# Cross attentions: maximum, subtraction, exponential and copy of turned weights on two PSUM banks at a time in place of one

## The reference

```python
scores = jnp.einsum('bhqd,bhkd->bhqk', qh, kh) / jnp.sqrt(jnp.float32(d_k))
attn = jax.nn.softmax(scores, axis=-1)
out = jnp.einsum('bhqk,bhkd->bhqd', attn, vh)
```

## Time and profile before

| | before |
|---|---|
| median of 3 runs | 1664.79 us (1664.47 to 1664.91) |
| profiled execution, its own time | 1663.43 us |
| its span | 1661.6 us |
| PE busy | 1302.8 us (78%) |
| DVE busy | 940.4 us (57%) |
| ACT busy | 737.3 us (44%) |
| POOL busy | 416.1 us (25%) |
| granted clock of PE, mean | 0.854 of full speed |

### The profile page before, as it was taken

One profiled execution on the slowest core, in us unless ns is written; L12 is line 12 of the kernel. 1 busy time (PEld: TensorE's weight loads), 2 busy tenths in 40 slices (PEclk: granted clock), 3 DMA queues, 4 the chain that ended last, 5 costly groups with the idle time before them and its releaser, 6 DMA issues. The chain is left out here.

```text
span 1661.6 us, 26970 instructions
## 1 busy us (share of the span) xinstructions
PE 1302.8 (78%) x9634; PEld 905.2 (54%) x9635; DVE 940.4 (57%) x2049; ACT 737.3 (44%) x1366; POOL 416.1 (25%) x435
## 2 busy tenths in 40 slices
PE   6997894468797975778778738693999768697998
PEld 3786463247464651346446527462677646365676
DVE  3687464767575456876775783485233367555111
ACT  2343552341462234675585534472455434163432
POOL 0222100013200015463463501300444335410000
PEclk9899797567797986879979967796999879798999
DMA  6000000200000000000000000510000000000000
GB/s 248 1 0 0 1 2 1 78 1 0 1 2 1 1 1 0 0 2 1 1 1 1 1 1 2 234 50 1 1 0 0 1 1 1 1 2 1 1 1 14
DMA packets 6340, 27.28 MB, mean 16 GB/s; under 512 B 1329, under 2 KB 4433, under 8 KB 5585
## 3 DMA queue, kind: packets, MB, share of 16 engines
q1 hardware_dynamic: 6224, 25.76, 3.9%
HBM read 25.23 MB, written 0.52 MB: 16 GB/s over the span
## 5 line engine op out<-in xcount | busy, mean ns | idle before, releaser
L745 DVE TENSOR_REDUCE L_xattn_top<-banks 128x4 f32<-128x512 f32 x128 | 80.7, 672 | 52.9 <-PE banks L603 52.9
L1188 DVE SCALAR_TENSOR_TENSOR L_ffn_a<-banks,L_ffn_act_out 128x512 f32<-128x512 f32 (+1 forms) x72 | 47.7, 662 | 103.5 <-POOL L_ffn_act_out L1118 99.8
L1118 POOL TENSOR_TENSOR L_ffn_act_out<-L_ffn_act_out,L_ffn_combine 128x512 f32<-128x512 f32 (+1 forms) x72 | 71.7, 996 | 77.9 <-ACT L_ffn_act_out L1164 77.9
L1132 PE MATMUL banks<-region_a,L_ffn_hs 128*128 128x512 f32 x144 | 72.9, 590 | 16.6 <-POOL L_ffn_hs L1111 15.4
L750 DVE TENSOR_TENSOR L_xattn_p<-banks,L_xattn_top 128x512 f32<-128x512 f32 x128 | 82.5, 686 | 4.8
L700 ACT ACTIVATE L_xattn_p<-L_xattn_p 128x512 f32<-128x512 f32 x128 | 75.8, 630 | 18.3 <-DVE L_xattn_p L750 18.2
L492 PE MATMUL banks<-w_const,h 128*128 128x128 f32 x96 | 24.8, 422 | 74.4 <-DVE h L487 74.4
L1164 ACT ACTIVATE L_ffn_act_out<-banks 128x512 f32<-128x512 f32 (+1 forms) x72 | 41.3, 574 | 90.3 <-PE banks L1132 90.3
L708 ACT ACTIVATE L_xattn_pT<-banks 128x512 f32<-128x512 f32 x128 | 69.7, 595 | 20.0 <-PE banks L616 20.0
L603 PE MATMUL banks<-L_xattn_ks,L_xattn_qT 32*128 32x512 f32 x256 | 76.6, 702 | 1.6 <-ACT L_xattn_qT L689 1.6
L616 PE MATMUL banks<-w_const,L_xattn_p 128*128 128x128 f32 x512 | 69.5, 278 | 6.2 <-ACT L_xattn_p L700 6.2
(11 more groups left out here) (502 smaller groups left out, 3404.6 us busy)
## 6 DMA issues: line engine op xcount, KB each, us to landing
region_b<-in_L_ffn SPq DMA_DIRECT2D x1, 6216.0 KB, 27.7
region_a<-in_L_ffn SPq DMA_DIRECT2D x1, 4416.0 KB, 13.6
region_b<-in_L_attn SPq DMA_DIRECT2D x1, 3150.5 KB, 10.4
region_a<-in_L_ffn SPq DMA_DIRECT2D x1, 3080.5 KB, 21.1
region_b<-in_L_attn SPq DMA_DIRECT2D x1, 1633.5 KB, 9.1
region_b<-in_L_xattn SPq DMA_DIRECT2D x1, 835.0 KB, 9.6
w_tables<-in_tables SPq DMA_DIRECT2D x1, 832.0 KB, 12.5
region_b<-in_L_ffn SPq DMA_DIRECT2D x1, 768.0 KB, 11.0
```

What stands on the lines that cost most here:

```text
L745: nc.vector.tensor_reduce(top[:, i, :], rows_of(score[i][:], 4), X, ALU.max)
L1118: nc.gpsimd.tensor_tensor(rows, rows, bc(combine[:, n, EXPERTS * q:EXPERTS * q + ex], 2, HALF // EXPERTS), ALU.mult).then_inc(weighed, 1)
L1132: nc.tensor.matmul(up[e][:, 0:widths[q]], hs[:, u, :], w["up"][:, up_at[q]:up_at[q] + widths[q]], start=True, stop=True).then_inc(hidden, 1)
L1188: nc.vector.scalar_tensor_tensor(a[:, e, 0:wide], up[e][:, 0:wide], 0.0, act_out[:, e, 0:wide], ALU.max, ALU.mult).then_inc(scaled, 1)
```

## The change

`center`, `weigh` and `keep` handle a pair with one instruction where there were two: one maximum over 128x1024 elements, one subtraction, one exponential, one copy of both turned banks. The same number of elements is handled. The semaphores count pairs instead of banks: the reduction waits for the scores of both banks; `turn(P)` waits once, for the exponential of the whole pair and for the copy of the whole pair before, and reports once, after its eighth transpose. No instruction changes its place in any queue.

```diff
@@ scores, turn, mix_values (PE)
                 if n >= 1:
-                    pe.wait_ge(centered, 2 * (P - 2) + 2)
+                    pe.wait_ge(centered, P - 1)
...
             def turn(P):
                 if P == 0:
                     pe.wait_ge(q_kept, 2)
+                pe.wait_ge(exped, P + 1)
+                if P >= 1:
+                    pe.wait_ge(pT_kept, P)
                 for e in range(2):
                     m = 2 * P + e
-                    pe.wait_ge(exped, m + 1)
-                    if m >= 2:
-                        pe.wait_ge(pT_kept, m - 1)
                     for s in range(4):
                         last = nc.tensor.transpose(tps[e][:, s * T:(s + 1) * T], p[:, m % 4, s * T:(s + 1) * T], g.ident)
-                    last.then_inc(turned, 1)
+                last.then_inc(turned, 1)
 
             def mix_values(n):
-                pe.wait_ge(pT_kept, 4 * n + 4)
+                pe.wait_ge(pT_kept, 2 * n + 2)
@@ weigh, keep (ACT)
             def weigh(P):
-                for m in (2 * P, 2 * P + 1):
-                    act.wait_ge(centered, m + 1)
-                    nc.scalar.activation(p[:, m % 4, :], p[:, m % 4, :], ACT.Exp, scale=scale).then_inc(exped, 1)
+                both = p[:, 2 * (P % 2):2 * (P % 2) + 2, :]
+                act.wait_ge(centered, P + 1)
+                nc.scalar.activation(both, both, ACT.Exp, scale=scale).then_inc(exped, 1)
...
-                for e in range(2):
-                    act.wait_ge(turned, 2 * P + e + 1)
-                    nc.scalar.activation(pT[:, n % 2, 2 * (P % 2) + e, :], tps[e][:], ACT.Copy).then_inc(pT_kept, 1)
+                act.wait_ge(turned, P + 1)
+                nc.scalar.activation(pT[:, n % 2, 2 * (P % 2):2 * (P % 2) + 2, :], g.banks[:, 4:6, :], ACT.Copy).then_inc(pT_kept, 1)
@@ center (DVE)
-                groups = (2 * (P % 2), 2 * (P % 2) + 1)
-                for e, i in enumerate(groups):
-                    dve.wait_ge(scored, 2 * P + e + 1)
-                    nc.vector.tensor_reduce(top[:, i, :], rows_of(score[i][:], 4), X, ALU.max)
+                i = 2 * (P % 2)
+                by_head = lambda t: t[:, i:i + 2, :].rearrange("p i (r k) -> p (i r) k", r=4)
+                tops = top[:, i:i + 2, :].rearrange("p i r -> p (i r)")
+                dve.wait_ge(scored, 2 * P + 2)
+                nc.vector.tensor_reduce(tops, by_head(g.banks), X, ALU.max)
                 dve.drain()
-                for e, i in enumerate(groups):
-                    if P >= 2:
-                        dve.wait_ge(turned, 2 * (P - 2) + e + 1)
-                    nc.vector.tensor_tensor(rows_of(p[:, i, :], 4), rows_of(score[i][:], 4), bc(top[:, i, :], 2, T),
-                                            ALU.subtract).then_inc(centered, 1)
+                if P >= 2:
+                    dve.wait_ge(turned, P - 1)
+                nc.vector.tensor_tensor(by_head(p), by_head(g.banks), bc(tops, 2, T), ALU.subtract).then_inc(centered, 1)
```

## The result

The changed kernel takes 1691.88 us (median of 4 runs, 1686.96 to 1693.01) against 1664.63 of the kernel before beside it on the same chip (4 runs, 1663.92 to 1664.91): ratio 1.0159, 95% interval 1.0138 to 1.0179. It is 27 us slower. The profiled execution took 1691.33, its span is 1689.5, 27.9 more than before. The merged instructions did what they say, and each engine but PE has less to do.

What follows compares the result with a forecast made beforehand. PE sets the pace, with the PE-ACT-PE round trip between transposes already as long as PE's own work. Added waits of 6.2, 7.4, 7.7 and 5.2 us in L0 to L3 sum to 26.5, giving 1691.3 us, range 1682 to 1703.

Steps and rivals of the forecast that it cites:

- The distance: Cross attentions, start of even to start of odd pair's transposes, through ACT's copy and exponential: 3.28 us instead of 2.41.
- PE's own work: What PE does anyway between even and odd transposes, subtracted from 3.28: 2.41 us in L1 and L2, 2.58 L0, 2.84 L3.
- The odd to even half: From the odd transposes to the next even ones in L1: stays covered, at 4.46 us.
- The chance that this half becomes late: After the odd transposes: mixing's copy ready at 2.34 us, mixing at 2.58; next even pair's exponential has 1.1 us left.
- The tails: End of each of four cross attentions: last mixing 5.56 us after last even transposes instead of 4.27, +1.29 each.
- Sum of the chains: Four cross attentions' added waits: L0 6.2, L1 7.4, L2 7.7, L3 5.2, together 26.5 us with the stage starts.
- The starts: Beginning of L2 and L3, where PE waits for the very first exponential, now wide: +0.34 us each.
- The clock: Rises of the granted clock shift between stages, up to 2 us each; 6 us added to each side of the range.
- a stage without an edit changing by over 2 us: Sign, in stages such as the feed-forward parts: a length change above 2 us means the sum is off.
- DVE and the clock in the bodies: Two rivals: DVE's two-bank instructions at half rate gate, 1777 us, 4 in 100; clock falls through bodies, 1890, 2 in 100.
- The columns: ACT's wide instructions: 0.17 us fixed plus 0.82 ns a column, so exponential 1.05 and copy 1.02 us.
- Banks: Skill rule against the change: ACT read bank 4 while PE wrote bank 5; now it waits for both, 0.51 us.

Runs made afterwards that it cites:

- on_path_wide: Kernel before with only odd pairs' exponentials and even pairs' copies wide, those between even and odd transposes: 1686.68 us, ratio 1.0153.
- after_again: The changed kernel without any edit, measured once more on another set of runs: 1688.28 us, ratio 1.0150 to the kernel before.
- max_sub_wide: Kernel before with only DVE's maximum and subtraction over two banks, exponentials and copies one bank each: 1663.54 us, ratio 0.9999.
- copy_wide: Kernel before with only ACT's copy of the turned weights over two banks: 1677.39 us, ratio 1.0088.
- off_path_wide: Kernel before with only even pairs' exponentials and odd pairs' copies wide, those not between even and odd transposes: 1668.58 us, ratio 1.0030.
- delay_6: Kernel before plus six extra DVE copies at the end of L0's cross attention, a pure shift: 1669.53 us, ratio 1.0039.
- delay_3: Kernel before plus three extra DVE copies at the end of L0's cross attention, a pure shift: 1664.94 us, ratio 1.0012.

## Why the prediction was right, and where not

The forecast was 1691.3, the time 1691.88. The mechanism is the one forecast, and its steps can be checked one by one:

- **The distance** was put at 3.28 in all four stages and is 3.21, from the third sequence on (3.09 to 3.15 in the first two). The step that was off is the copy's start: four transposes were counted as half of the 1.02 between starts, 0.51; the wide copy started 1.19 after the transposes, so they are 0.44. Eight of them are then 0.88; the other 0.14 of the 1.02 lies between the last transpose and the scores. The exponential's start 0.92 later (forecast 0.91), its 1.05 (1.05) and the 0.05 to PE were right. That PE's own work is to be subtracted held, and on_path_wide pays the same wait with half as many wide instructions. But 2.41, 2.58 and 2.84 are too small by some 0.10 each: they end at the odd pair's weight load, which starts while PE still does the turned sums, and the 3.28 is where its first matmul starts. By matmuls PE's own work is 2.51, 2.68 and 2.95.
- **The odd to even half** was to stay 4.46, and is 4.38 (4.87 became 4.81 in L0 and L3). Most of that gain is the other side of the same 0.10, for by matmuls the half went from 4.36 to 4.38 and from 4.76 to 4.81. In L1 and L2 a break of 0.05 us ahead of the second bank's transposes is also gone, since they no longer wait for a second exponential. The chance that this half becomes late did not arise: mixing comes 2.50 after the odd transposes.
- **The tails** were to grow by 1.29 each and grew by 1.15 (5.42 instead of 4.27): twice the 0.07 of the copy's start.
- **Sum of the chains.** These three make 26.5 - 0.7 (the starts) = 25.8 into 21.7, 4.1 us less than forecast. L1 and L2 cost 0.72 a sequence instead of 0.87 in 12 sequences, which is 1.8 (the first sequence of each cost 0.88, as forecast). The 14 sequences of L0 and L3 cost 0.13 less each on average, another 1.8, and the four tails 0.14 less each (0.6).
- **The starts** of L2 and L3 were put at 0.34. In both the exponential's part is 0.43. L2's start as a whole lost 1.8, since L582 and the context's projection ran at the lower clock; L3's became 0.4 shorter.
- **The clock** was left out of the sum and given 6 us to either side. What is neither chain nor wide exponential came out at +5.3 us in the profiled execution (27.9 - 21.7 - 0.9), with about 1.4 (L2's start), 2 x 1.4 (the tails of L0 and L2) and 2.6 (the last stage), less what other stages gained. That the clock is behind it is shown for these places only. That it about made up for the chain's missing 4 us is chance. A forecast with the right chain and no clock would have been 1687, which is nearer to after_again's 1688.28. I had also written that a stage without an edit changing by over 2 us would put the sum off: one did, by 2.60.
- **DVE and the clock in the bodies.** 1198 and 1225 ns, as assumed; max_sub_wide shows no price. The bodies stayed at 1.00 with PE idle for 0.54 us in 7.59. The swing of the clock that the Trainium skill reports for another kernel with short idle times between groups of matmuls ("TensorE: Matmul & The Clock Gate", A second HAM failure mode: psum-queue depth-cycling) did not show at that size. Two of the four tails, with longer idle times, did drop, to 0.59 and 0.55.
- **The columns.** The wide exponential took 1052 ns and the wide copy 1023. The Trainium skill's 186 ns + 0.833 ns a column ("ScalarE: Activation LUTs", What ACT_TABLE_LOAD costs) gives 1039, as an estimate, so this case agrees within 16 ns.
- **Banks.** copy_wide, with only the copy waiting for both banks, cost 0.38 us a sequence in L1 and 11.0 over the chains. The Trainium skill's rule to read from another bank than the one being written ("PSUM — Partial Sum Buffer", Summary: rules for kernel authors) points the right way here, for the reason that the trace shows: the reader can start on the first while the second is being filled.

## What to carry to other kernels

Merging two instructions of an engine that isn't the bound saved 0.06 to 0.10 us here, where it is worth nothing, and took away the overlap of producer and consumer between the two halves. That cost 0.38 us in each sequence of L1 for the copy alone, 0.35 for the exponential alone and 0.72 for both. No run kept the halves and made them wait for the whole pair, so the single wait and the single instruction are shown only together. For a change of this kind, look first at which engine waits next for the merged result, and at how long its own work until then lasts. Where that was longer than the merged chain (the odd copies and the even exponentials here, or L3's 2.84 us against one wide instruction), the merge cost nothing; where it was just as long, 0.72 of the added 0.80 us was paid. And before work is moved to cover a wait, follow each result that moves with it through the queues of the other engines; here a cover for 0.54 us made a new wait of 1.00.

## What the runs showed of the hardware

- ACT reading two PSUM banks in one instruction costs no more than its columns: 1023 ns for 1024 columns against 595 for 512. DVE's wide reduction took 1198 and its wide subtraction 1225 ns, where a pair of halves takes 1.22 and 1.29 us from start to end.
- All four tails of the changed kernel have the same shape: PE idle for 1.78 to 2.01 us ahead of the last transposes and for 0.89 ahead of the last mixing, after bodies at 1.00. In L0 and L2 the granted clock of the mixing was 0.59 and 0.55, in L1 and L3 1.00. In after_again L2's tail, with the same idle times, had 1.00. The idle time alone doesn't decide it: off_path_wide's L0 tail had 0.54 after 1.21 and 0.89 us, while the four tails of copy_wide kept 1.00 after 1.36 to 1.58 and 0.89.
- Some of the edited kernels vary more from run to run: delay_6 over 7.5 us in 4 runs, the changed kernel over 16 us in 6, but delay_3 only over 3.3 in 10; the kernel before over 1.0 us in 4 runs, 3.5 in 11 and 5.8 in 23. The chains in the profiles repeat to 0.03 us, so the spread comes from elsewhere; which stages carry it in the runs without a profile stays open.
